# A GRU recurrence: the kept share on GpSimd, gates by the sigmoid, one joined low half, and another order of TensorE's products

## The chip, the cores and the metric

The program runs on one core of a Trainium2 chip. The metric is the device time of one execution in microseconds (us), lower is better. TensorE's granted clock is given as a share of full speed: 1.00 is 2.4 GHz, 0.50 is 1.2 GHz.

## The reference, cut to what matters

The whole reference is four layers one after the other, each added to its input: a GRU scan, an attention layer, a layer of experts and a second attention layer. Only the GRU scan is touched by the change. It walks over 196 places (14 x 14) in order, with 16 images and 192 channels at each:

```python
def step(h, xz):
    h_zrn = h @ Wh.T + bh
    x_z, x_r, x_n = jnp.split(xz, 3, axis=-1)
    h_z, h_r, h_n = jnp.split(h_zrn, 3, axis=-1)
    z = jax.nn.sigmoid(x_z + h_z)
    r = jax.nn.sigmoid(x_r + h_r)
    ncand = jnp.tanh(x_n + r * h_n)
    h_new = (1.0 - z) * ncand + z * h
    return (h_new, h_new)
_, hs = jax.lax.scan(step, h0, x_zrn_t)
```

Each step needs the state of the step before, so the 196 steps form one chain.

## The kernel before

The function `gru` holds one program for each engine, and all of them loop over the T = 196 steps. The 16 images stand in the free dimension, the 192 channels in two blocks of partitions, so every elementwise tile is 128 x 32. Work on a step goes round in a ring.

TensorE adds up three sums in PSUM: `ps_r` for the reset gate, `ps_n` for the candidate, `ps_z` for the update gate. It starts them with nine products that do not depend on the state (L516 to L518), and adds the products of the state with the recurrent weights through `gate` (L499, its matmul is L502). The state is scaled and kept as fp16 parts, a high one and a low one that holds the rest. A high part costs 6 small products, a low one 4. To start early, the new state is not awaited as a whole: it is a sum of a kept share z*h and a new share (1-z)*ncand, and `ps_r` and `ps_n` take the parts of each share (KEPT_HIGH, KEPT_LOW, NEW_HIGH, NEW_LOW) as they come, while `ps_z` takes the parts of their sum (SUM_HIGH, SUM_LOW).

ScalarE forms `tr` (L557) when `r_summed` is up, `tz` (L559) when `z_summed` is up, and the candidate `n` (L561). Both gates are a tanh of half the argument, so VectorE must add 1 and halve where it uses them.

VectorE forms `rn` (L467) from `tr` and `ps_n`, `cand` (L469), then KEPT_HIGH (L474), `zc` (L475), `kept` (L476), NEW_HIGH (L479), `new` (L480), KEPT_LOW (L483), NEW_LOW (L486), SUM_HIGH (L487), the state itself (L488), SUM_LOW (L491) and half of the state (L492). All these tiles except `ps_n` are in SBUF. GpSimd has nothing to do in the loop.

Every engine works through its own list in the order of the code. Where an instruction waits for two things, the code has two waits ahead of it:

```python
dve.wait_ge(tr_ready, t + 1)
dve.wait_ge(n_summed, t + 1)
dve.scalar_tensor_tensor(rn[:, b, :], tr[:, b, :], 1.0, ps_n[:, b, :2 * B], ALU.add, ALU.mult).then_inc(rn_ready, 1)
```

Of the kernel before, what the change touches and what calls it, by code (L numbers as in the profile page):

```python
# [2232 lines left out]
```

## Time and profile before

| what | value |
|---|---|
| median of 3 runs | 1899.13 us (1893.85 to 1899.2) |
| the profiled execution, its own time | 1891.38 us |
| its span, first to last instruction | 1889.6 us |
| mean granted clock of TensorE | 0.795 |
| busy over the span: TensorE, VectorE, ScalarE, GpSimd | 79%, 70%, 50%, 39% |
| TensorE products, the group of the costliest GRU line (`ps_r`, L502) | 3920, mean 176 ns |

The shares of the whole span mix four layers. What the change can be worth has to be read from the stretch of the recurrence alone, and there from a single step, since all steps are alike.

### The profile page before, as it was taken

To read this page: it belongs to the slowest core of one execution; us is meant where nothing else is said; L and a number is where in the kernel's file an instruction comes from. 1 tells how busy PE (TensorE), PEld (TensorE's weight loads), DVE (VectorE), ACT (ScalarE), POOL (GpSimd) and SP (SyncE) were. 2 spreads that over 40 slices of the span, in tenths; PEclk is the share of its full clock that TensorE was granted. 3 is DMA by queue.
4 is the path that set the end of the run, shared out by engine and by line. 5 is a ranking of instruction groups with operands and counts; after the bars stand their busy time and mean duration, and the time that the engine had idled before them with its cause. 6 is when DMAs were issued, how large, how long until landed. Compare 5 with 4: busy or idle time off the path is not lost. (4 is left out here: it accounts for less than half of the span.)

```text
span 1889.6 us, 51642 instructions
## 1 busy us (share of the span) xinstructions
PE 1499.0 (79%) x19499; PEld 1285.8 (68%) x19499; DVE 1322.3 (70%) x4846; ACT 952.1 (50%) x1920; POOL 740.8 (39%) x676
## 2 busy tenths in 40 slices
PE   4778888888853888888877799599992597887887
PEld 4667777777743776767666577488881586676766
DVE  7888888888867567878766765244446746787874
ACT  4633333333333567878725235244432456787872
POOL 3700000000004056869843013355540415686994
PEclk9955555555576899999985699799995689999998
DMA  3000000000022696767325214322215459676832
GB/s 83 4 4 4 4 5 4 4 4 5 4 67 85 168 246 133 158 129 148 58 59 167 77 40 163 113 64 65 65 56 158 132 148 241 136 157 126 150 58 59
DMA packets 62927, 167.59 MB, mean 89 GB/s; under 512 B 16680, under 2 KB 40344, under 8 KB 59996
## 3 DMA queue, kind: packets, MB, share of 16 engines
q1 hardware_dynamic: 57308, 151.44, 32.2%
q0 software_dynamic: 5376, 12.85, 2.3%
q8 instruction: 159, 2.61, 0.6%
q14 instruction: 84, 0.69, 0.1%
HBM read 96.24 MB, written 67.42 MB: 87 GB/s over the span
## 5 line engine op out<-in xcount | busy, mean ns | idle before, releaser
L983 POOL TENSOR_TENSOR l_arena<-l_arena,l_arena 98x784 fp32r<-98x784 f32 x192 | 354.7, 1860 | 113.3 <-PE l_ps L1092 69.6
L502 PE MATMUL gru_ps_r<-gru_hp,gru_wp 128*128 128x16 f16 x3920 | 200.5, 176 | 70.4 <-DVE gru_hp L474 69.6
L502 PEld LDWEIGHTS gru_ps_r<-gru_hp,gru_wp 128*128 128x128 f16 x3920 | 150.9, 105 | 92.0 <-DVE gru_hp L474 90.0
L922 POOL MEMSET l_arena<- 32x6272 f32 x2 | 10.6, 5320 | 513.0 <-POOLq L45 513.0
L1266 DVE TENSOR_REDUCE l_ps<-l_ps 98x4 f32<-98x784 f32 x192 | 187.5, 977 | 28.1 <-PE l_ps L1053 23.0
L502 PE MATMUL gru_ps_n<-gru_hp,gru_wp 128*128 128x16 f16 x3920 | 191.2, 174 | 0.0
L1091 PE MATMUL l_ps<-l_arena,l_arena 128*66 128x196 f32 x768 | 163.6, 266 | 25.0 <-POOL l_arena L983 24.7
L557 ACT ACTIVATE gru_tr<-gru_ps_r,gru_unscale 128x32 f32<-128x32 f32 x196 | 56.4, 288 | 220.5 <-PE gru_ps_r L502 220.5
L1206 ACT ACTIVATE l_arena<-l_ps 98x784 fp32r<-98x784 f32 x192 | 158.4, 825 | 4.6
L1209 ACT ACTIVATE l_arena<-l_ps 98x784 f32<-98x784 f32 x192 | 157.0, 818 | 0.0
L1092 PE MATMUL l_ps<-l_arena,l_arena 128*66 128x196 f32 x768 | 156.8, 257 | 0.0
L502 PEld LDWEIGHTS gru_ps_n<-gru_hp,gru_wp 128*128 128x128 f16 x3920 | 150.0, 104 | 0.0
L1197 ACT ACTIVATE l_arena<-l_ps 2x392 fp32r<-2x392 f32 x192 | 94.1, 490 | 100.7 <-PE l_ps L1062 94.3
L1053 PE MATMUL l_ps<-l_arena,l_arena 128*98 128x196 f32 x768 | 113.8, 272 | 33.2 <-DMA l_arena<-l_arena 18.9
L1091 PEld LDWEIGHTS l_ps<-l_arena,l_arena 128*66 128x66 f32 x768 | 107.5, 140 | 43.9 <-POOL l_arena L983 31.6
L1053 PEld LDWEIGHTS l_ps<-l_arena,l_arena 128*98 128x98 f32 x768 | 87.1, 171 | 52.0 <-DVE l_mt L1273 25.3
L1240 DVE COPY l_arena<-l_ps 64x196 f32<-64x196 f32 x192 | 67.6, 352 | 61.5 <-PE l_ps L1092 58.7
L1092 PEld LDWEIGHTS l_ps<-l_arena,l_arena 128*66 128x66 f32 x768 | 108.2, 141 | 1.2
L1074 PE MATMUL l_ps<-l_arena,l_arena 128*98 128x196 f32 x768 | 104.1, 259 | 0.0
L2043 DVE TENSOR_TENSOR l_arena<-mx_ps,l_arena 128x512 fp32r<-128x512 f32 x56 | 38.7, 692 | 79.2 <-ACT l_arena L1875 75.8
L1693 POOL DMA_INDIRECT picked<-l_arena,mx_target x56 | 55.3, 987 | 93.2 <-DVE l_arena L2049 93.2
L1038 PE MATMUL l_ps<-l_arena,l_arena 128*56 128x224 f32 x168 | 60.0, 357 | 38.2 <-DVE l_arena L1232 35.5
(365 smaller groups left out, 4649.3 us busy)
## 6 DMA issues: line engine op xcount, KB each, us to landing
l_arena<-qk SPq DMA_DIRECT2D x48, 588.0 KB
qk<-l_arena SPq DMA_DIRECT2D x48, 392.0 KB, 6.9
rel<-l_arena SPq DMA_DIRECT2D x24, 686.0 KB
l_arena<-rel SPq DMA_DIRECT2D x24, 686.0 KB
l_arena<-x SPq DMA_DIRECT2D x32, 294.0 KB, 7.6
qk<-l_arena SPq DMA_DIRECT2D x12, 784.0 KB, 14.2
l_arena<-in_experts_dram SPq DMA_DIRECT2D x8, 1152.0 KB, 7.5
l_arena<-picked SPq DMA_DIRECT2D x16, 294.0 KB
```

The lines of the kernel that those rows point to most:

```text
L502: last = pe.matmul(out[:, b, B * m:B * m + B], wp[:, wi, g, m, :], hp[:, b, part, B * k:B * k + B], start=False, stop=True, skip_group_che ...
L983: pool.tensor_tensor(pl[:TH, g % 2, :, :], p32[:TH, g % 2, :, :], ph[:TH, g % 4, :, :].bitcast(f32), ALU.subtract).then_inc(pl_ready, 1)
L1038: pe.matmul(out, rh[:, n, :], line(high), start=True, stop=False)
L1053: last = pe.matmul(ps[:TH, S_BANK + head, half * T:half * T + T], q[:, head, queries], k[:, head, keys], start=True, stop=True)
L1074: last = pe.matmul(ps[:TH, T_BANK + 2 * (g % 2) + head, half * T:half * T + T], k[:, head, keys], q[:, head, queries], start=True, stop=True)
L1091: pe.matmul(out, values, ph[:, g % 4, head, cols], start=head == 0 and keys == 0, stop=False)
L1092: last = pe.matmul(out, values, pl[:, g % 2, head, cols], start=False, stop=head == 1 and keys == 1)
L1197: act.activation(q[0:2, :, b * T:(b + 1) * T], ps[64:66, R_BANK, :TB].rearrange("p (h t) -> p h t", h=2), ACT.Copy).then_inc(x_copied, 1)
L1206: act.activation(ph[:TH, g % 4, :, :], banks, ACT.Exp).then_inc(p_high, 1)
L1209: act.activation(p32[:TH, g % 2, :, :], banks, ACT.Exp).then_inc(p_ready, 1)
L1240: dve.tensor_copy(o_quad[p // 2][row:row + 64, b * T:(b + 1) * T], ps[:64, O_BANK, :T]).then_inc(o_kept, 1)
L1266: dve.tensor_reduce(m, ps[:TH, S_BANK:S_BANK + 2, :TB].rearrange("p c (h k) -> p c h k", h=2), AXIS.X, ALU.max).then_inc(mx_ready, 1)
```

## The change

In the loop of `gru`, five things change.

- ScalarE forms the gates `reset` and `keep` by the sigmoid in place of tanh. VectorE no longer adds 1 and halves; `unscale` loses its factor of one half, and the tile `half` becomes `held`, the whole state.
- GpSimd forms the kept share `kept` (a product of `keep` and the state) and its rest KEPT_LOW. VectorE did both before.
- For the candidate's sum the two low parts are added to a single part, BOTH_LOW, by a new VectorE instruction; TensorE multiplies it once (4 products) where it multiplied KEPT_LOW and NEW_LOW (8 products).
- `renew` (formerly `zc`), `new` and `held` (formerly `half`) lie in PSUM, in a bank of their own called `shares`.
- TensorE's products come in another order.

```diff
-        hp = s.sb("hp", [128, 2, 6, 2 * B], fp16)
+        hp = s.sb("hp", [128, 2, 7, 2 * B], fp16)
...
-        tr, tz, zc, rn, cand, tn, kept, new, half = (s.sb(n, [128, 2, 2 * B]) for n in names)
+        reset, keep, rn, cand, tn, kept = (s.sb(n, [128, 2, 2 * B]) for n in names)
...
+        shares = s.ps("shares", 1)[:, 0, :12 * B].rearrange("p (a b n) -> p a b n", a=3, b=2)
+        renew, new, held = (shares[:, a] for a in range(3))
...
-                    dve.wait_ge(tr_ready, t + 1)
+                    dve.wait_ge(reset_ready, t + 1)
                     dve.wait_ge(n_summed, t + 1)
-                    dve.scalar_tensor_tensor(rn[:, b, :], tr[:, b, :], 1.0, ps_n[:, b, :2 * B], ALU.add, ALU.mult).then_inc(rn_ready, 1)
+                    dve.tensor_tensor(rn[:, b, :], reset[:, b, :], ps_n[:, b, :2 * B], ALU.mult).then_inc(rn_ready, 1)
...
-                    dve.wait_ge(tz_ready, t + 1)
-                    dve.wait_ge(half_ready, t + 1)
-                    dve.scalar_tensor_tensor(hp[:, 1 - b, KEPT_HIGH, :], tz[:, b, :], 1.0, half[:, b, :], ALU.add, ALU.mult).then_inc(kept_high, 1)
-                    dve.tensor_scalar(zc[:, b, :], tz[:, b, :], -0.5 * HSCALE, 0.5 * HSCALE, ALU.mult, ALU.add).then_inc(zc_ready, 1)
-                    dve.scalar_tensor_tensor(kept[:, b, :], tz[:, b, :], 1.0, half[:, b, :], ALU.add, ALU.mult).then_inc(kept_ready, 1)
-                    dve.wait_ge(zc_ready, t + 1)
+                    dve.wait_ge(keep_ready, t + 1)
+                    dve.wait_ge(held_ready, t + 1)
+                    dve.tensor_tensor(hp[:, 1 - b, KEPT_HIGH, :], keep[:, b, :], held[:, b, :], ALU.mult).then_inc(kept_high, 1)
+                    dve.tensor_scalar(renew[:, b, :], keep[:, b, :], -HSCALE, HSCALE, ALU.mult, ALU.add).then_inc(renew_ready, 1)
+                    dve.wait_ge(renew_ready, t + 1)
                     dve.wait_ge(tn_ready, t + 1)
-                    dve.tensor_tensor(hp[:, 1 - b, NEW_HIGH, :], zc[:, b, :], tn[:, b, :], ALU.mult).then_inc(new_high, 1)
-                    dve.tensor_tensor(new[:, b, :], zc[:, b, :], tn[:, b, :], ALU.mult).then_inc(new_ready, 1)
-                    dve.wait_ge(kept_high, t + 2)
-                    dve.wait_ge(kept_ready, t + 1)
-                    dve.tensor_tensor(hp[:, 1 - b, KEPT_LOW, :], kept[:, b, :], hp[:, 1 - b, KEPT_HIGH, :], ALU.subtract).then_inc(kept_low, 1)
+                    dve.tensor_tensor(hp[:, 1 - b, NEW_HIGH, :], renew[:, b, :], tn[:, b, :], ALU.mult).then_inc(new_high, 1)
+                    dve.tensor_tensor(new[:, b, :], renew[:, b, :], tn[:, b, :], ALU.mult).then_inc(new_ready, 1)
                     dve.wait_ge(new_high, t + 2)
                     dve.wait_ge(new_ready, t + 1)
                     dve.tensor_tensor(hp[:, 1 - b, NEW_LOW, :], new[:, b, :], hp[:, 1 - b, NEW_HIGH, :], ALU.subtract).then_inc(new_low, 1)
+                    dve.wait_ge(kept_ready, t + 1)
                     dve.tensor_tensor(hp[:, 1 - b, SUM_HIGH, :], new[:, b, :], kept[:, b, :], ALU.add).then_inc(sum_high, 1)
                     dve.tensor_tensor(state[:, t + 1, :, :], two(new[:, b, :]), two(kept[:, b, :]), ALU.add).then_inc(h_ready, 1)
+                    dve.wait_ge(new_low, t + 2)
+                    dve.wait_ge(kept_low, t + 2)
+                    dve.tensor_tensor(hp[:, 1 - b, BOTH_LOW, :], hp[:, 1 - b, KEPT_LOW, :], hp[:, 1 - b, NEW_LOW, :], ALU.add).then_inc(both_low, 1)
...
-                    dve.tensor_scalar(two(half[:, 1 - b, :]), state[:, t + 1, :, :], 0.5, None, ALU.mult).then_inc(half_ready, 1)
+                    dve.tensor_tensor(held[:, 1 - b, :], new[:, b, :], kept[:, b, :], ALU.add).then_inc(held_ready, 1)
...
                     gate(ps_r, 1, b, NEW_HIGH)
-                    gate(ps_n, 2, b, NEW_HIGH)
                     pe.wait_ge(kept_low, t + 1)
                     gate(ps_r, 1, b, KEPT_LOW)
+                    gate(ps_n, 2, b, NEW_HIGH, [0])
                     pe.wait_ge(new_low, t + 1)
                     gate(ps_r, 1, b, NEW_LOW).then_inc(r_summed, 1)
-                    gate(ps_n, 2, b, KEPT_LOW)
-                    gate(ps_n, 2, b, NEW_LOW).then_inc(n_summed, 1)
+                    gate(ps_n, 2, b, NEW_HIGH, [1])
                     pe.wait_ge(sum_high, t + 1)
                     gate(ps_z, 0, b, SUM_HIGH)
+                    pe.wait_ge(both_low, t + 1)
+                    gate(ps_n, 2, b, BOTH_LOW).then_inc(n_summed, 1)
                     pe.wait_ge(sum_low, t + 1)
...
+                for t in range(T):
+                    b = t % 2
+                    pool.wait_ge(h_ready, t + 1)
+                    pool.wait_ge(keep_ready, t + 1)
+                    pool.tensor_tensor(two(kept[:, b, :]), two(keep[:, b, :]), state[:, t, :, :], ALU.mult).then_inc(kept_ready, 1)
+                    pool.wait_ge(kept_high, t + 2)
+                    pool.wait_ge(kept_ready, t + 1)
+                    pool.tensor_tensor(hp[:, 1 - b, KEPT_LOW, :], kept[:, b, :], hp[:, 1 - b, KEPT_HIGH, :], ALU.subtract).then_inc(kept_low, 1)
...
-                    act.activation(tr[:, b, :], ps_r[:, b, :2 * B], ACT.Tanh, scale=unscale[:, 0:1]).then_inc(tr_ready, 1)
+                    act.activation(reset[:, b, :], ps_r[:, b, :2 * B], ACT.Sigmoid, scale=unscale[:, 0:1]).then_inc(reset_ready, 1)
...
-                    act.activation(tz[:, b, :], ps_z[:, b, :2 * B], ACT.Tanh, scale=unscale[:, 0:1]).then_inc(tz_ready, 1)
+                    act.activation(keep[:, b, :], ps_z[:, b, :2 * B], ACT.Sigmoid, scale=unscale[:, 0:1]).then_inc(keep_ready, 1)
```

TensorE, one step, the products that depend on the state, before. In this code `x6` stands for six products in a row; they are in turn KEPT_HIGH for both sums, NEW_HIGH for both, then both low parts for `ps_r` (x8), both low parts for `ps_n` (x8), and the sum's parts for `ps_z` (x10).

```order
L502 MATMUL gru_ps_r<-gru_hp,gru_wp 128x16 x6
L502 MATMUL gru_ps_n<-gru_hp,gru_wp 128x16 x6
L502 MATMUL gru_ps_r<-gru_hp,gru_wp 128x16 x6
L502 MATMUL gru_ps_n<-gru_hp,gru_wp 128x16 x6
L502 MATMUL gru_ps_r<-gru_hp,gru_wp 128x16 x8
L502 MATMUL gru_ps_n<-gru_hp,gru_wp 128x16 x8
L502 MATMUL gru_ps_z<-gru_hp,gru_wp 128x16 x10
```

The same place after the change. The `x10` are NEW_HIGH (6) and KEPT_LOW (4), the `x4` behind the first `x3` is NEW_LOW, and the last `ps_n` group is BOTH_LOW.

```order
L504 MATMUL gru_ps_r<-gru_hp,gru_wp 128x16 x6
L504 MATMUL gru_ps_n<-gru_hp,gru_wp 128x16 x6
L504 MATMUL gru_ps_r<-gru_hp,gru_wp 128x16 x10
L504 MATMUL gru_ps_n<-gru_hp,gru_wp 128x16 x3
L504 MATMUL gru_ps_r<-gru_hp,gru_wp 128x16 x4
L504 MATMUL gru_ps_n<-gru_hp,gru_wp 128x16 x3
L504 MATMUL gru_ps_z<-gru_hp,gru_wp 128x16 x6
L504 MATMUL gru_ps_n<-gru_hp,gru_wp 128x16 x4
L504 MATMUL gru_ps_z<-gru_hp,gru_wp 128x16 x4
```

Between the last product of `ps_r` and the last of `ps_n` there stood 8 products, and now there stand 13. The count of a step goes from 50 to 46.

VectorE, one step from KEPT_HIGH on, before:

```order
L474 SCALAR_TENSOR_TENSOR gru_hp<-gru_tz,gru_half 128x32
L475 TENSOR_SCALAR gru_zc<-gru_tz 128x32
L476 SCALAR_TENSOR_TENSOR gru_kept<-gru_tz,gru_half 128x32
L479 TENSOR_TENSOR gru_hp<-gru_zc,gru_n 128x32
L480 TENSOR_TENSOR gru_new<-gru_zc,gru_n 128x32
L483 TENSOR_TENSOR gru_hp<-gru_kept,gru_hp 128x32
L486 TENSOR_TENSOR gru_hp<-gru_new,gru_hp 128x32
L487 TENSOR_TENSOR gru_hp<-gru_new,gru_kept 128x32
L488 TENSOR_TENSOR l0s_state<-gru_new,gru_kept 128x32
L491 TENSOR_TENSOR gru_hp<-l0s_state,gru_hp 128x32
L492 TENSOR_SCALAR gru_half<-l0s_state 128x32
```

And after (`gru_shares` is the PSUM tile with `renew`, `new` and `held`; L490 is BOTH_LOW):

```order
L476 TENSOR_TENSOR gru_hp<-gru_keep,gru_shares 128x32
L477 TENSOR_SCALAR gru_shares<-gru_keep 128x32
L480 TENSOR_TENSOR gru_hp<-gru_shares,gru_n 128x32
L481 TENSOR_TENSOR gru_shares<-gru_shares,gru_n 128x32
L484 TENSOR_TENSOR gru_hp<-gru_shares,gru_hp 128x32
L486 TENSOR_TENSOR gru_hp<-gru_shares,gru_kept 128x32
L487 TENSOR_TENSOR l0s_state<-gru_shares,gru_kept 128x32
L490 TENSOR_TENSOR gru_hp<-gru_hp 128x32
L493 TENSOR_TENSOR gru_hp<-l0s_state,gru_hp 128x32
L494 TENSOR_TENSOR gru_shares<-gru_shares,gru_kept 128x32
```

`kept` and KEPT_LOW have left the list, and BOTH_LOW has come in between the state and SUM_LOW.

## Rows read from the trace of the kernel before

**Rows 1.** Busy time by stretch: recurrence, and the stage ahead; x counts instructions

```profile
core 0: us, PE busy (x) PEld busy (x) DVE busy (x) ACT busy (x) POOL busy (x), PEclk, DMA share, GB/s
107.00:530.00 423.00, 351.00 (x11425) 329.06 (x11422) 363.77 (x2527) 155.42 (x582) 0.00 (x0) 0.50 0.02 4
...
0.00:90.00 90.00, 56.16 (x292) 53.39 (x292) 71.17 (x195) 48.43 (x98) 49.42 (x38) 0.99 0.16 44
```

**Rows 2.** Waits, 110 to 530 us: total, times, longest

```profile
ACT gru_tr L557 <- PE gru_ps_r L502: 214.6, 193, 1.4
```

**Rows 3.** Timeline of VectorE over one step: start us, length us

```profile
507.20 0.19 DVE L479 TENSOR_TENSOR gru_hp<-gru_zc,gru_n 128x32 f16<-128x32 f32 x1
507.31 0.19 DVE L480 TENSOR_TENSOR gru_new<-gru_zc,gru_n 128x32 f32<-128x32 f32 x1
...
507.60 0.19 DVE L486 TENSOR_TENSOR gru_hp<-gru_new,gru_hp 128x32 f16<-128x32 f32 x1
...
507.81 0.18 DVE L488 TENSOR_TENSOR l0s_state<-gru_new,gru_kept 128x32 f32<-128x32 f32 x1
508.10 0.19 DVE L491 TENSOR_TENSOR gru_hp<-l0s_state,gru_hp 128x32 f16<-128x32 f32 x1
...
508.51 0.19 DVE L467 SCALAR_TENSOR_TENSOR gru_rn<-gru_tr,gru_ps_n 128x32 f32<-128x32 f32 x1
508.74 0.25 DVE L469 SCALAR_TENSOR_TENSOR gru_cand<-gru_rn,gru_unscale,l0g_cand_in 128x32 f32<-128x32 f32 x1
508.99 0.19 DVE L474 SCALAR_TENSOR_TENSOR gru_hp<-gru_tz,gru_half 128x32 f16<-128x32 f32 x1
...
509.36 0.19 DVE L479 TENSOR_TENSOR gru_hp<-gru_zc,gru_n 128x32 f16<-128x32 f32 x1
```

**Rows 4.** Timeline of TensorE's weight loads, one row of the step

```profile
507.44 0.24 PEld L502 LDWEIGHTS gru_ps_r<-gru_hp,gru_wp 128*128 128x128 f16 x6
```

**Rows 5.** Timeline of TensorE's products, same step: first start, length to last end

```profile
507.45 0.33 PE L502 MATMUL gru_ps_r<-gru_hp,gru_wp 128*128 128x16 f16 x6
507.63 0.31 PE L502 MATMUL gru_ps_n<-gru_hp,gru_wp 128*128 128x16 f16 x6
507.79 0.36 PE L502 MATMUL gru_ps_r<-gru_hp,gru_wp 128*128 128x16 f16 x8
508.01 0.36 PE L502 MATMUL gru_ps_n<-gru_hp,gru_wp 128*128 128x16 f16 x8
508.22 0.41 PE L502 MATMUL gru_ps_z<-gru_hp,gru_wp 128*128 128x16 f16 x10
508.49 0.19 PE L516 MATMUL gru_ps_r<-l0g_gates_in,gru_ident 128*128 128x32 bf16 x1
```

**Rows 6.** Timeline of ScalarE, same step, with idle time and releaser

```profile
508.19 0.29 ACT L557 ACTIVATE gru_tr<-gru_ps_r,gru_unscale 128x32 f32<-128x32 f32 x1 [1.10 <-PE gru_ps_r L502]
508.67 0.29 ACT L559 ACTIVATE gru_tz<-gru_ps_z,gru_unscale 128x32 f32<-128x32 f32 x1 [0.19 <-PE gru_ps_z L502]
509.02 0.23 ACT L561 ACTIVATE gru_n<-gru_cand 128x32 f32<-128x32 f32 x1
```

**Rows 7.** Timeline of GpSimd in a later layer, two dependent instructions

```profile
735.23 0.21 POOL L967 CAST l_rec_parts<-l_sums 98x32 fp32r<-98x32 f32 x1
735.52 0.25 POOL L969 TENSOR_TENSOR l_rec_parts<-l_sums,l_rec_parts 98x32 fp32r<-98x32 f32 x1
```

**Rows 8.** Groups by shape: busy us, mean ns, idle before

```profile
L961 POOL TENSOR_TENSOR l_arena<-l_arena,l_arena 98x128 fp32r<-98x128 f32 x96 | 40.3, 440 | 0.0
...
L1431 ACT ACTIVATE ro_std<-ro_var_sums,ro_eps 128x32 f32<-128x32 f32 x1 | 0.3, 287 | 6.7 <-PE ro_var_sums L1406 6.7
```

**Rows 9.** VectorE groups by shape, inputs in SBUF, then one in PSUM

```profile
L1901 DVE TENSOR_TENSOR mx_key<-l_logits,mx_m 98x256 f32<-98x256 f32 x2 | 0.8, 425 | 0.1
...
L1932 DVE TENSOR_TENSOR mx_pos<-mx_ps,mx_base_slot 98x256 f32<-98x256 f32 x1 | 0.4, 424 | 0.0
```

**Rows 10.** Line 168: min/median/max ns; result in SBUF, then in PSUM

```profile
L168 DVE TENSOR_SCALAR l_arena<-l_arena,l_arena x64: 364/375/3690, 591.3 to 1513.6; 96x196 f32<-96x196 f32 x64
L168 DVE TENSOR_SCALAR gi_xn<-l_x,gi_rstd,gi_shift x32: 453/473/493, 21.8 to 73.6; 96x196 f32<-96x196 f32 x32
```

More of the change, by code:

```diff
@@ L388, in gru @@
         bp, br = s.sb("bp", [128, 3, 2, B], bf16), s.sb("br", [128, 2, B])
-        hp = s.sb("hp", [128, 2, 6, 2 * B], fp16)
-        KEPT_HIGH, KEPT_LOW, NEW_HIGH, NEW_LOW, SUM_HIGH, SUM_LOW = range(6)
-        names = "tr tz zc rn cand n kept new half".split()
-        tr, tz, zc, rn, cand, tn, kept, new, half = (s.sb(n, [128, 2, 2 * B]) for n in names)
+        hp = s.sb("hp", [128, 2, 7, 2 * B], fp16)
+        KEPT_HIGH, KEPT_LOW, NEW_HIGH, NEW_LOW, SUM_HIGH, SUM_LOW, BOTH_LOW = range(7)
+        names = "reset keep rn cand n kept".split()
+        reset, keep, rn, cand, tn, kept = (s.sb(n, [128, 2, 2 * B]) for n in names)
         ps_r, ps_n, ps_z = s.ps("ps_r", 2), s.ps("ps_n", 2), s.ps("ps_z", 2)
+        shares = s.ps("shares", 1)[:, 0, :12 * B].rearrange("p (a b n) -> p a b n", a=3, b=2)
+        renew, new, held = (shares[:, a] for a in range(3))
         wo_raw = s.sb("wo_raw", [128, 2, CB, CP])
@@ L400, in gru @@
         kept_high, kept_low, new_high, new_low = (s.sem(n) for n in ("kept_high", "kept_low", "new_high", "new_low"))
-        h_ready, half_ready, sum_high, sum_low = (s.sem(n) for n in ("h_ready", "half_ready", "sum_high", "sum_low"))
+        h_ready, held_ready, sum_high, sum_low, both_low = (s.sem(n) for n in ("h_ready", "held_ready", "sum_high", "sum_low", "both_low"))
         r_summed, n_summed, z_summed = s.sem("r_summed"), s.sem("n_summed"), s.sem("z_summed")
-        tr_ready, tz_ready, tn_ready = s.sem("tr_ready"), s.sem("tz_ready"), s.sem("tn_ready")
-        zc_ready, rn_ready, cand_ready = s.sem("zc_ready"), s.sem("rn_ready"), s.sem("cand_ready")
+        reset_ready, keep_ready, tn_ready = s.sem("reset_ready"), s.sem("keep_ready"), s.sem("tn_ready")
+        renew_ready, rn_ready, cand_ready = s.sem("renew_ready"), s.sem("rn_ready"), s.sem("cand_ready")
         kept_ready, new_ready = s.sem("kept_ready"), s.sem("new_ready")
@@ L420, in _ @@
                 dve.memset(state[:, 0, :, :], 0.0).then_inc(h_ready, 1)
-                dve.memset(half[:, 0, :], 0.0).then_inc(half_ready, 1)
+                dve.memset(held[:, 0, :], 0.0).then_inc(held_ready, 1)
                 for part, ready in ((KEPT_HIGH, kept_high), (KEPT_LOW, kept_low), (NEW_HIGH, new_high), (NEW_LOW, new_low),
-                                    (SUM_HIGH, sum_high), (SUM_LOW, sum_low)):
+                                    (SUM_HIGH, sum_high), (SUM_LOW, sum_low), (BOTH_LOW, both_low)):
                     dve.memset(hp[:, 0, part, :], 0.0).then_inc(ready, 1)
@@ L440, in _ @@
                 link(dve.tensor_scalar(power[:, :].bitcast(mybir.dt.uint32), largest[:, :].bitcast(mybir.dt.uint32), 0x7F800000, None, ALU.bitwise_and))
-                link(dve.tensor_scalar(unscale[:, :], power[:, :], 0.5 / HSCALE * 2.0 ** -13, None, ALU.mult))
+                link(dve.tensor_scalar(unscale[:, :], power[:, :], 1.0 / HSCALE * 2.0 ** -13, None, ALU.mult))
                 dve.reciprocal(scale[:, :], power[:, :]).then_inc(scale_ready, 1)
@@ L497, in _, with gate @@
                 LOW = [(0, 0), (2, 1)]
-                def gate(out, g, b, part):
-                    for m in range(2):
+                def gate(out, g, b, part, halves=range(2)):
+                    for m in halves:
                         for wi, k in HIGH if part in (KEPT_HIGH, NEW_HIGH, SUM_HIGH) else LOW:
```

## The prediction

> **What bounds the kernel now.** I first read busy time by stretch. The recurrence lasts from 107 to 530 us, 423 us of the span, or 2.16 us for each of 196 steps; TensorE has its lower clock all through (0.50, 1.2 GHz) and is busy 351 us of it, so no engine is full [rows 1]. The waits then say who waits: ScalarE waits for the reset gate's sums, 1.1 us in each of 193 steps [rows 2]. That is a ring, not a full engine, so I read one step of the timeline and followed the ring from NEW_HIGH (L479) to the next NEW_HIGH. All times below are us after the start of NEW_HIGH at 507.20.
>
> - NEW_HIGH ends at 0.19 [rows 3]; TensorE's weight load for it starts at 0.24 [rows 4], the first product at 0.25.
> - 20 products later (6 + 6 + 8) the sums of `ps_r` end at 0.95 (507.79 + 0.36) [rows 5].
> - ScalarE starts `tr` at 0.99 and ends it at 1.28 [rows 6]; `rn` starts at 1.31, `cand` at 1.54 and ends at 1.79 [rows 3]; `n` starts at 1.82 and ends at 2.05 [rows 6]; the next NEW_HIGH starts at 2.16 [rows 3], or 2.15 without the rounding.
>
> Nothing on this ring stands idle: each starts 0.03 to 0.11 after the end of the one before. The other branches come out close behind. `rn` also needs the candidate's sums, which end at 1.17 (508.01 + 0.36) [rows 5]. The gate `tz` ends at 1.76, and KEPT_HIGH starts at 1.79 [rows 6, 3]; its 12 products are through just before NEW_HIGH is there.
>
> Three prices for the sum. Products follow at 0.027 (from 507.63 to 508.49 there are 6 + 8 + 8 + 10 = 32 of them in 0.86), the first group after a pause takes about 0.02 more (507.45 to 507.63 against 507.63 to 507.79), and a product ends 0.17 to 0.18 after its start (the last of the 6 that begin at 507.63 starts 0.135 later and ends at 0.31) [rows 5]. Independent VectorE instructions start 0.10 to 0.11 apart. A dependent one starts 0.04 after its producer's end if it has one wait (`rn` ends 508.70, `cand` 508.74), but 0.10 to 0.11 if it has two and the one written second comes last (`new` ends 507.50, L486 starts 507.60; L488 ends 507.99, L491 starts 508.10) [rows 3]. `rn` before waits for `tr` first and `n_summed` second, and the second is there long ahead, so it starts 0.03 after `tr`.
>
> **The change, part by part.**
>
> *Products.* 4 fewer in a step would be 0.11 us if TensorE were full. It isn't; what counts is where the last product of each sum stands. NEW_HIGH is ready for TensorE at 0.24 as before. Then come 6 + 4 + 3 products, and the weight load for NEW_LOW could be at about 0.25 + 0.02 + 13 x 0.027 = 0.62, less a little since loads run ahead: 0.60. NEW_LOW itself: `new` starts 0.11, ends 0.30, plus 0.10 for the second wait, plus 0.19 is 0.59, plus 0.05 to the load is 0.64. So TensorE now pauses 0.04 there, where 20 products covered it before. The products of NEW_LOW start at 0.65 and, with 0.02 for the restart, 4 of them put the next one at 0.78; the last ends at 0.75 + 0.17 = 0.92 to 0.93. The reset gate is ready 0.02 to 0.03 earlier than before: `reset` ends 0.96 + 0.29 = 1.25, and `rn` could start at 1.28.
>
> *The candidate's sums.* Behind the last product of `ps_r` now stand 3 + 6 + 4 = 13 products in place of 8. They end at 0.93 + 13 x 0.027 = 1.28, against 1.17. BOTH_LOW doesn't delay them: VectorE reaches it at 0.40 + 0.11 + 0.10 + 0.10 = 0.71, it ends at 0.90, is ready for TensorE at 0.95, and its turn is at 0.78 + 9 x 0.027 = 1.02. Now `n_summed` is the last wait of `rn`, and it is written second: 1.28 + 0.10 = 1.38. Against 1.31 that is **+0.07 us a step**. Before, the same edge would have given 1.17 + 0.10 = 1.27, 0.04 ahead of the reset gate: the cover was thin, and the five products use it up. The price of the second wait is bounded by the rows at 0.04 and 0.11; I take 0.10, since it is the same form of code.
>
> *Sigmoid for tanh.* No sigmoid of this shape runs before. Another function at 128 x 32 from PSUM, the square root, takes 287 ns [rows 8], as the tanh's 0.29 [rows 6], so I take no difference. If it took 0.05 more, `reset` would be ready at 1.33, still inside 1.38. `rn` becomes a product of two tensors, no shorter on VectorE (0.18 to 0.19 for either kind) [rows 3].
>
> *GpSimd.* `keep` ends at about 1.75: the state starts 0.21 after NEW_LOW's 0.40, ends at 0.79, and SUM_LOW with its second wait (0.10), 0.19 and 0.05 is there for TensorE at 1.13; the last of its 4 products ends at 1.42, then 0.04 and 0.29. GpSimd forms `kept` from perhaps 1.87 to 2.12 (0.25 for 98 x 32; 0.08 from one dependent instruction to the next) and KEPT_LOW from 2.20 to 2.45 [rows 7]. With 0.05 it is ready at 2.50; its turn in a step of 2.22 is at 2.22 + 0.24 + 0.18 = 2.64. So it is hidden with 0.14 to spare under the products of the state. VectorE's two instructions less save nothing, as it had gaps. If each took the 440 ns of a 98 x 128 tile [rows 8], KEPT_LOW would be 0.24 late and cost up to that a step; the near row is the 98 x 32 one, so I take nothing.
>
> *Tiles in PSUM.* Only `new` and what reads it lie on the path. A PSUM input costs nothing for a product of two tensors: 424 ns against 425 at 98 x 256 [rows 9]. A PSUM result does for L168, 473 ns against 375 [rows 10]. If that were a fixed price, `new` would be 0.10 later; if it goes by columns (196 there, 32 here) it is 0.016. I take nothing, as that line has one tensor input and `new` has two. The Trainium skill, VectorE: DVE Perf Modes, section on the perf-mode tier table, says that fp32 `tensor_scalar` runs at twice the rate in SBUF only, while `tensor_tensor` has the single rate in either memory. By that rule L168's 98 ns are the lost rate and `new` pays nothing; by the row read as a fixed price the sum would be +0.17 a step.
>
> *The sum.* 0.07 us x 196 = 13.7 us, made against the profiled execution's own 1891.4 us: 1905.1. That execution lies 7.7 us under the median of the runs, 1899.1; on the median the forecast is **1912.8 us**. Rounding of the rows (0.01 at three joints) is worth 2 us either way. Other layers aren't touched.
>
> **The rivals.**
>
> 1. *The candidate's edge is cheaper, and the change is a wash.* If `new` is done 0.04 earlier in PSUM, TensorE doesn't pause: all 30 products to the last of `ps_n` run from 0.25, ending at 0.25 + 0.02 + 29 x 0.027 + 0.17 = 1.22, and `rn` starts at 1.32, +0.01: 1901. If only the second wait costs 0.04, `rn` starts at 1.32 too. For it: both are thin margins. Against: rows show 0.10 twice, and no PSUM result that was faster. Chance 0.18, 1895 to 1904.
> 2. *Faster.* VectorE's instructions with a PSUM operand are shorter throughout. It decides once NEW_HIGH, with `renew` now in PSUM, is at least 0.015 shorter and `new` and NEW_LOW together 0.05: then the whole run of products moves up. With 0.06 off each of the three, the products begin at 0.19, `rn` starts at 1.26, and with `rn` itself 0.02 shorter a step is 0.07 less: 1885. Against it: the pair of 424 and 425 ns. Chance 0.18, 1880 to 1893.
> 3. *Much slower.* GpSimd is late, or `new` pays the 0.10 of L168. Either gives some 0.10 more a step, 1932. For it: no GpSimd row has this shape with waits on two other engines, and its instructions sit in the ring of KEPT_LOW, `ps_r` and `keep`. Against: 0.14 of slack. Chance 0.14, 1920 to 1945.
>
> The same page of the skill, section on the TRN2 errata, gives VectorE a fixed part of 120 cycles from PSUM and 58 from SBUF. By it `new` and NEW_LOW would each take 62 cycles at 0.96 GHz, 65 ns, longer, an estimate of +0.13 a step on top of mine, in rival 3's direction; the pair of 424 and 425 ns disagrees, and rival 3 would keep its chance without it.
>
> **How the numbers follow.** The forecast has a chance of 0.50, with 1904 to 1920 as its own range (second wait 0.07 to 0.11, rounding, some of the columns' 0.016). A measurement here tells no change from change beyond 0.3%, 5.7 us or 0.03 us a step. Slower is then 0.50 + 0.14 = 0.64, same 0.18, faster 0.18. The range from 1893 to 1928 takes in the forecast and the wash and most of a GpSimd that is only a little late, and leaves out the faster case and the worst of the third.
>
> **What would show it.** In the timeline of a step: the period 2.22 us in place of 2.15; the last product of `ps_n` ending 0.35 after the last of `ps_r` (0.22 before); `rn` starting 0.13 after `reset` ends, not 0.03, and VectorE's idle time ahead of it put down to TensorE, not to ScalarE; a pause of 0.04 ahead of NEW_LOW's products; the recurrence 13 to 14 us longer, and everything behind it as before. `new` at 0.19, the sigmoid at 0.29, GpSimd's two at 0.25 each would confirm the prices. I am wrong if `new` or NEW_HIGH is clearly shorter in PSUM, if `rn` starts within 0.05 of the candidate's sums, if TensorE's first wait after NEW_HIGH is on GpSimd, or if the clock in the stretch isn't 0.50.

## The result, and the profile after

The changed kernel takes 1908.94 us, the median of 9 runs (1904.54 to 1914.37); the kernel before, run beside it, 1893.85 us (9 runs, 1888.44 to 1899.2). The ratio is 1.008 with a 95% interval of 1.0061 to 1.0098, so it is slower by 0.8%, 15 us. The forecast was slower by 0.07 us a step, 13.7 us; its 1912.8 us is counted from 1899.13, the median of 3 runs of the kernel before.

The profiled execution spans 1907.1 us at a mean clock of 0.791. Where does the length lie? One instruction stands once in each of the 196 steps, `rn`. This view gives its shortest, median and longest duration in ns, and its first and last start in us; the line under it says how long VectorE sat idle ahead of it, how often, and for whom. It counts only pauses above 0.15 us.

```profile
L469 DVE TENSOR_TENSOR gru_rn<-gru_reset,gru_ps_n x196: 178/188/189, 104.5 to 542.0; 128x32 f32<-128x32 f32 x196
its engine sat idle before it (us, times) until:
  PE gru_ps_n L504: 37.1, 190
```

The same view of the kernel before:

```profile
L467 DVE SCALAR_TENSOR_TENSOR gru_rn<-gru_tr,gru_ps_n x196: 180/186/190, 103.5 to 528.1; 128x32 f32<-128x32 f32 x196
its engine sat idle before it (us, times) until:
  ACT gru_tr L557: 2.6, 4
```

From the first `rn` to the last are 437.5 us after and 424.6 before: 12.9 us more in 195 steps, 0.066 a step. The counts of 190 and 4 say who was awaited, but not how much longer: the pause before was 0.13 us in the typical step, just too short to be counted. The groups by shape give all of VectorE's idle time ahead of `rn` in the recurrence (the number behind the second bar), before and after:

```profile
L467 DVE SCALAR_TENSOR_TENSOR gru_rn<-gru_tr,gru_ps_n 128x32 f32<-128x32 f32 x193 | 36.1, 187 | 24.4 <-ACT gru_tr L557 0.7
L469 DVE TENSOR_TENSOR gru_rn<-gru_reset,gru_ps_n 128x32 f32<-128x32 f32 x193 | 36.2, 188 | 35.3 <-PE gru_ps_n L504 35.0
```

It rose from 0.13 to 0.18 us a step, and now it ends with TensorE's candidate sums.

The busy time by stretch, in the columns of [rows 1], first the recurrence, then a stretch of the untouched layers:

```profile
107.00:543.00 436.00, 364.10 (x10661) 333.07 (x10661) 335.05 (x2333) 156.06 (x584) 97.27 (x390) 0.50 0.02 4
...
887.00:1187.00 300.00, 260.14 (x1421) 198.65 (x1419) 206.18 (x483) 141.19 (x238) 125.84 (x117) 0.80 0.36 99
```

and the matching later stretch of the kernel before:

```profile
873.00:1173.00 300.00, 254.07 (x1430) 194.59 (x1429) 208.56 (x484) 143.29 (x241) 125.19 (x117) 0.83 0.35 98
```

In the recurrence the granted clock is 0.50, as in [rows 1], so the clock has no part in the 12.9 us. The spans differ by 17.5 us: 12.9 in the steps, 1.0 ahead of the first `rn`, and 3.6 behind the last, where nothing was changed and one execution had 0.80 where the other had 0.83. Those 3.6 us can't be put down to the change: in the profiled executions of this document, all with the same later layers, the stretch behind the last `rn` takes from 1358.6 to 1372.1 us. Between the medians of 9 runs the difference is 15.1.

One step of the changed kernel on VectorE, in the columns of [rows 3]; a bracket gives the idle time ahead and what ended it:

```profile
507.07 0.19 DVE L480 TENSOR_TENSOR gru_hp<-gru_shares,gru_n 128x32 f16<-128x32 f32 x1 [0.17 <-ACT gru_n L572]
507.18 0.19 DVE L481 TENSOR_TENSOR gru_shares<-gru_shares,gru_n 128x32 f32<-128x32 f32 x1
507.47 0.19 DVE L484 TENSOR_TENSOR gru_hp<-gru_shares,gru_hp 128x32 f16<-128x32 f32 x1
...
507.77 0.16 DVE L490 TENSOR_TENSOR gru_hp<-gru_hp 128x32 f16<-128x32 f16 x1
...
508.45 0.19 DVE L469 TENSOR_TENSOR gru_rn<-gru_reset,gru_ps_n 128x32 f32<-128x32 f32 x1 [0.18 <-PE gru_ps_n L504]
508.67 0.25 DVE L471 SCALAR_TENSOR_TENSOR gru_cand<-gru_rn,gru_unscale,l0g_cand_in 128x32 f32<-128x32 f32 x1
...
509.29 0.19 DVE L480 TENSOR_TENSOR gru_hp<-gru_shares,gru_n 128x32 f16<-128x32 f32 x1 [0.15 <-ACT gru_n L572]
```

TensorE's products of the step, in the columns of [rows 5]:

```profile
507.32 0.44 PE L504 MATMUL gru_ps_r<-gru_hp,gru_wp 128*128 128x16 f16 x10
507.61 0.23 PE L504 MATMUL gru_ps_n<-gru_hp,gru_wp 128*128 128x16 f16 x3
507.72 0.28 PE L504 MATMUL gru_ps_r<-gru_hp,gru_wp 128*128 128x16 f16 x4
507.85 0.23 PE L504 MATMUL gru_ps_n<-gru_hp,gru_wp 128*128 128x16 f16 x3
507.93 0.31 PE L504 MATMUL gru_ps_z<-gru_hp,gru_wp 128*128 128x16 f16 x6
508.09 0.25 PE L504 MATMUL gru_ps_n<-gru_hp,gru_wp 128*128 128x16 f16 x4
```

ScalarE and GpSimd in the same step:

```profile
508.03 0.29 ACT L568 ACTIVATE gru_reset<-gru_ps_r,gru_unscale 128x32 f32<-128x32 f32 x1 [1.07 <-PE gru_ps_r L504]
508.53 0.29 ACT L570 ACTIVATE gru_keep<-gru_ps_z,gru_unscale 128x32 f32<-128x32 f32 x1 [0.21 <-PE gru_ps_z L504]
508.96 0.23 ACT L572 ACTIVATE gru_n<-gru_cand 128x32 f32<-128x32 f32 x1
```

```profile
508.96 0.25 POOL L555 TENSOR_TENSOR gru_kept<-gru_keep,l0s_state 128x32 f32<-128x32 f32 x1 [1.61 <-ACT gru_keep L570]
509.35 0.25 POOL L558 TENSOR_TENSOR gru_hp<-gru_kept,gru_hp 128x32 f16<-128x32 f32 x1
```

The step is 2.22 us long (509.29 less 507.07), as in the median over the recurrence, against 2.15. The last product of `ps_r` ends at 508.00 (507.72 + 0.28), the last of `ps_n` at 508.34 (508.09 + 0.25): 0.34 behind it. `reset` ends at 508.32, and `rn` starts at 508.45, 0.13 later and 0.11 behind the candidate's sums. The reset gate alone would have let it go at 508.35, 0.03 behind its end, as `rn` started behind `tr` before [rows 3, 6].

### The profile page after: what moved, and what is told of

Same layout as the page of the kernel before. It is cut to its first block and busy times, and to the rows that moved or that the text cites. A ratio compares the mean times of both kernels' runs of the same rounds, so it can differ in the third digit from the quotient of the medians.

```text
span 1907.1 us, 50662 instructions
## 1 busy us (share of the span) xinstructions
PE 1518.7 (80%) x18715; PEld 1292.6 (68%) x18715; DVE 1291.4 (68%) x4651; ACT 952.9 (50%) x1920; POOL 839.7 (44%) x1068
## 5 line engine op out<-in xcount | busy, mean ns | idle before, releaser
L504 PE MATMUL gru_ps_n<-gru_hp,gru_wp 128*128 128x16 f16 x3136 | 199.1, 174 | 0.0
L555 POOL TENSOR_TENSOR gru_kept<-gru_keep,l0s_state 128x32 f32<-128x32 f32 x196 | 49.6, 253 | 322.7 <-ACT gru_keep L570 322.7
L568 ACT ACTIVATE gru_reset<-gru_ps_r,gru_unscale 128x32 f32<-128x32 f32 x196 | 56.4, 288 | 214.3 <-PE gru_ps_r L504 214.3
L504 PEld LDWEIGHTS gru_ps_n<-gru_hp,gru_wp 128*128 128x128 f16 x3136 | 144.2, 104 | 0.5
L504 PE MATMUL gru_ps_z<-gru_hp,gru_wp 128*128 128x16 f16 x1960 | 109.8, 176 | 0.7 <-DVE gru_hp L493 0.7
```

What stands on the lines that cost most here:

```text
L504: last = pe.matmul(out[:, b, B * m:B * m + B], wp[:, wi, g, m, :], hp[:, b, part, B * k:B * k + B], start=False, stop=True, skip_group_che ...
L568: act.activation(reset[:, b, :], ps_r[:, b, :2 * B], ACT.Sigmoid, scale=unscale[:, 0:1]).then_inc(reset_ready, 1)
```

## The experiments

Three explanations had to be told apart. By the prediction's, `rn` waits for the candidate's sums, which now come 13 products behind those of the reset gate, and the wait for them is written second, which costs 0.10 in place of 0.04. Or the loss lies in the other parts (GpSimd, sigmoid, PSUM). Or the late sums are the cause, but by their lateness alone, and where their wait is written costs nothing of its own. The first four kernels ran beside a kernel before with a median of 1893.46 us, the last four beside one of 1894.69 us. "A typical step" is the median over the recurrence of one profiled execution. Before: 2.15, after: 2.22.

### e1: the order undone

The changed kernel with TensorE's order of before and without BOTH_LOW; GpSimd, the sigmoid and the PSUM tiles stay.

```diff
-                    dve.wait_ge(new_low, t + 2)
-                    dve.wait_ge(kept_low, t + 2)
-                    dve.tensor_tensor(hp[:, 1 - b, BOTH_LOW, :], hp[:, 1 - b, KEPT_LOW, :], hp[:, 1 - b, NEW_LOW, :], ALU.add).then_inc(both_low, 1)
...
                     gate(ps_r, 1, b, NEW_HIGH)
+                    gate(ps_n, 2, b, NEW_HIGH)
                     pe.wait_ge(kept_low, t + 1)
                     gate(ps_r, 1, b, KEPT_LOW)
-                    gate(ps_n, 2, b, NEW_HIGH, [0])
                     pe.wait_ge(new_low, t + 1)
                     gate(ps_r, 1, b, NEW_LOW).then_inc(r_summed, 1)
-                    gate(ps_n, 2, b, NEW_HIGH, [1])
+                    gate(ps_n, 2, b, KEPT_LOW)
+                    gate(ps_n, 2, b, NEW_LOW).then_inc(n_summed, 1)
                     pe.wait_ge(sum_high, t + 1)
                     gate(ps_z, 0, b, SUM_HIGH)
-                    pe.wait_ge(both_low, t + 1)
-                    gate(ps_n, 2, b, BOTH_LOW).then_inc(n_summed, 1)
```

> The changed kernel with the products' order of before and without BOTH_LOW (both low parts are multiplied for the candidate's sum again); sigmoid, GpSimd's share and the tiles in PSUM stay. Theory (the place of the candidate's last product is the whole loss): a step of 2.15 to 2.16 us as before, rn 0.03 after reset, ratio to before 0.998 to 1.002. Rival (GpSimd, the tiles in PSUM or the sigmoid carry a good part of the loss): a step of 2.18 to 2.22 us, ratio 1.004 to 1.008.

Measured: 1895.74 us, ratio to before 1.0004 (0.9981 to 1.0027), a typical step 2.146 us. The view of `rn`:

```profile
L469 DVE TENSOR_TENSOR gru_rn<-gru_reset,gru_ps_n x196: 186/187/189, 105.3 to 527.2; 128x32 f32<-128x32 f32 x196
its engine sat idle before it (us, times) until:
  ACT gru_reset L564: 1.7, 1
```

From first to last are 421.9 us, 2.7 less than before, with GpSimd, the sigmoid and PSUM all in place. They cost nothing that shows within the interval, 0.3% at most. The whole loss goes with the order and BOTH_LOW.

### e2: the order alone

The kernel before with the new order of products and BOTH_LOW on VectorE; tanh, `half`, SBUF tiles and `kept` on VectorE stay.

```diff
+                    dve.wait_ge(new_low, t + 2)
+                    dve.wait_ge(kept_low, t + 2)
+                    dve.tensor_tensor(hp[:, 1 - b, BOTH_LOW, :], hp[:, 1 - b, KEPT_LOW, :], hp[:, 1 - b, NEW_LOW, :], ALU.add).then_inc(both_low, 1)
...
-                    gate(ps_n, 2, b, NEW_HIGH)
...
+                    gate(ps_n, 2, b, NEW_HIGH, [0])
...
-                    gate(ps_n, 2, b, KEPT_LOW)
-                    gate(ps_n, 2, b, NEW_LOW).then_inc(n_summed, 1)
+                    gate(ps_n, 2, b, NEW_HIGH, [1])
...
+                    pe.wait_ge(both_low, t + 1)
+                    gate(ps_n, 2, b, BOTH_LOW).then_inc(n_summed, 1)
```

> The kernel before with the new order of products and with BOTH_LOW on VectorE; tanh, kept and KEPT_LOW on VectorE and all tiles in SBUF stay. Theory: the whole loss, a step of 2.22 us, rn 0.10 after the last product of the candidate's sum ends, ratio to before 1.006 to 1.008. Rival (the loss is in the other parts): a step of 2.15 to 2.18 us, ratio under 1.004.

Measured: 1909.46 us, ratio 1.0084 (1.0061 to 1.0108), a typical step 2.22 us.

```profile
L467 DVE SCALAR_TENSOR_TENSOR gru_rn<-gru_tr,gru_ps_n x196: 179/186/190, 103.4 to 540.9; 128x32 f32<-128x32 f32 x196
its engine sat idle before it (us, times) until:
  PE gru_ps_n L505: 39.4, 188
```

437.5 us from first to last, the very length of the changed kernel, and the same wait in 188 steps. The ratio lies a hair above the expected 1.006 to 1.008, which its interval reaches. With e1 this settles where the loss is, and the explanation by the other parts falls.

### e3: the candidate's low part ahead of the update gate

The changed kernel with BOTH_LOW's products in front of SUM_HIGH's, so that 7 products stand behind the last of `ps_r` and not 13.

```diff
+                    pe.wait_ge(both_low, t + 1)
+                    gate(ps_n, 2, b, BOTH_LOW).then_inc(n_summed, 1)
                     pe.wait_ge(sum_high, t + 1)
                     gate(ps_z, 0, b, SUM_HIGH)
-                    pe.wait_ge(both_low, t + 1)
-                    gate(ps_n, 2, b, BOTH_LOW).then_inc(n_summed, 1)
```

> The changed kernel with the 4 products of BOTH_LOW ahead of the 6 of SUM_HIGH. Theory: BOTH_LOW is ready for TensorE 0.92 us after NEW_HIGH, so TensorE pauses there for 0.04, the candidate's sums end at 1.20 in place of 1.27, rn starts at 1.31; a step of 2.15 to 2.17 us (the update gate comes 0.05 later and may cost up to 0.015 through KEPT_LOW on GpSimd), ratio to before 0.999 to 1.003. Rival (the loss is not in the distance from the reset gate's last product to the candidate's): still 2.20 us or more, ratio 1.006 or more.

Measured: 1896.74 us, ratio 1.0008 (0.9988 to 1.0027), a typical step 2.15 us. Two rows of TensorE and `rn` in one step, from two timelines:

```profile
402.46 0.28 PE L504 MATMUL gru_ps_r<-gru_hp,gru_wp 128*128 128x16 f16 x4
402.59 0.42 PE L504 MATMUL gru_ps_n<-gru_hp,gru_wp 128*128 128x16 f16 x7
...
403.11 0.19 DVE L469 TENSOR_TENSOR gru_rn<-gru_reset,gru_ps_n 128x32 f32<-128x32 f32 x1
```

The sums of `ps_n` end 0.27 behind those of `ps_r` (403.01 and 402.74). Moving six products past four took the loss away with everything else left as it was. `rn` still starts 0.10 to 0.11 behind the candidate's sums, the price of the wait written second, but that is now only 0.04 behind the end of `reset` in the median (0.03 before, 0.13 in the changed kernel).

### e4: one wait for `rn`

The changed kernel, with both of `rn`'s producers raising one semaphore, so that there is a single wait.

```diff
-                    dve.wait_ge(reset_ready, t + 1)
-                    dve.wait_ge(n_summed, t + 1)
+                    dve.wait_ge(rn_inputs, 2 * t + 2)
...
-                    gate(ps_n, 2, b, BOTH_LOW).then_inc(n_summed, 1)
+                    gate(ps_n, 2, b, BOTH_LOW).then_inc(rn_inputs, 1)
...
-                    act.activation(reset[:, b, :], ps_r[:, b, :2 * B], ACT.Sigmoid, scale=unscale[:, 0:1]).then_inc(reset_ready, 1)
+                    act.activation(reset[:, b, :], ps_r[:, b, :2 * B], ACT.Sigmoid, scale=unscale[:, 0:1]).then_inc(rn_inputs, 1)
```

> The changed kernel with one semaphore for both inputs of rn (the reset gate and the candidate's sums both count it up, and rn waits once for the even value); nothing else changes. Theory (0.06 to 0.07 us of the loss is the price of the second of two waits): rn starts 0.04 after the candidate's sums end, or 0.03 after reset ends if that is later, at 1.31 in place of 1.38 after NEW_HIGH; a step of 2.15 to 2.16 us, ratio 0.998 to 1.002. Rival (0.10 is the time that any wait of VectorE for TensorE takes): no change against the changed kernel, a step of 2.22 us, ratio 1.007.

Measured: 1891.55 us, ratio 0.9989 (0.9972 to 1.0006), a typical step 2.15 us. The last product of `ps_n` and `rn` in one step, from two timelines of this kernel:

```profile
403.42 0.25 PE L503 MATMUL gru_ps_n<-gru_hp,gru_wp 128*128 128x16 f16 x4
...
403.71 0.19 DVE L468 TENSOR_TENSOR gru_rn<-gru_reset,gru_ps_n 128x32 f32<-128x32 f32 x1
```

The order is the slow one and the sums are as late as ever, ending at 403.67 (in the median 0.35 behind those of `ps_r`, as in the changed kernel); but `rn` starts 0.04 behind them, not 0.11. The kernel gains all of the 0.07 us back. So the loss has two conditions, and taking either away heals it: the sums must be last, and their wait must be the one written second. Lateness alone doesn't explain it.

### e5: the two waits of `rn` swapped

```diff
-                    dve.wait_ge(reset_ready, t + 1)
                     dve.wait_ge(n_summed, t + 1)
+                    dve.wait_ge(reset_ready, t + 1)
```

> The changed kernel with the two waits of rn in the other order: the candidate's sums first, reset second. Theory (the wait written second costs 0.10 from its producer's end, the one written first 0.04): rn starts 0.04 after the candidate's sums (1.31) or 0.10 after reset ends (1.25 + 0.10 = 1.35 to 1.36), whichever is later, so 1.36 and 0.10 after reset; a step of 2.20 us, ratio to before 1.004 to 1.006. Rival (the price is that of having two waits, in either order): rn stays at 1.38, a step of 2.22 us, ratio 1.007 to 1.008.

Measured: 1903.46 us, ratio 1.0042 (1.0022 to 1.0062), a typical step 2.19 us. The reset gate and `rn` in one step:

```profile
403.36 0.29 ACT L568 ACTIVATE gru_reset<-gru_ps_r,gru_unscale 128x32 f32<-128x32 f32 x1 [1.06 <-PE gru_ps_r L504]
...
403.75 0.19 DVE L469 TENSOR_TENSOR gru_rn<-gru_reset,gru_ps_n 128x32 f32<-128x32 f32 x1 [0.16 <-PE gru_ps_n L504]
```

The swap brings back 0.03 of the 0.07, and no more, because both inputs come within 0.02 of each other. In the compiled program the wait written second is an instruction of its own, ahead of `rn` in VectorE's queue; where its input is the late one, the trace records it 0.065 us before the instruction that it guards. Now it waits for the reset gate, which ends at 403.65, and `rn` follows at 403.75, 0.10 later. The bracket names TensorE here, since its sums ended 0.01 after the gate, yet with the waits this way round it is the gate that `rn` hangs on: a releaser named by the view is the input that came last, which isn't always the one that held the instruction.

### e6: every late wait alone or first

The changed kernel with e4's edit, the same for NEW_HIGH (whose inputs are `renew` and `n`), and the waits swapped where the late one was second: NEW_LOW, SUM_LOW, and GpSimd's KEPT_LOW. The order of products stays the slow one.

```diff
-                    dve.wait_ge(renew_ready, t + 1)
-                    dve.wait_ge(tn_ready, t + 1)
+                    dve.wait_ge(new_inputs, 2 * t + 2)
...
-                    dve.wait_ge(new_high, t + 2)
                     dve.wait_ge(new_ready, t + 1)
+                    dve.wait_ge(new_high, t + 2)
...
-                    dve.wait_ge(sum_high, t + 2)
                     dve.wait_ge(h_ready, t + 2)
+                    dve.wait_ge(sum_high, t + 2)
...
-                    pool.wait_ge(kept_high, t + 2)
                     pool.wait_ge(kept_ready, t + 1)
+                    pool.wait_ge(kept_high, t + 2)
```

> The changed kernel, its order of products kept; rn and NEW_HIGH wait once each on a shared semaphore, and NEW_LOW, SUM_LOW and KEPT_LOW on GpSimd have the wait that comes last written first. Theory: 0.06 to 0.07 us less at each of rn, NEW_HIGH and NEW_LOW, as far as another branch does not hold: NEW_HIGH 0.03 after n ends, NEW_LOW 0.04 after new ends, no pause of TensorE ahead of NEW_LOW; a step of 2.03 to 2.09 us, ratio to before 0.987 to 0.994. Rival (some engine is nearly full, so the time comes back elsewhere): a step of 2.13 us or more, ratio over 0.997.

Measured: 1866.22 us, ratio 0.9852 (0.9828 to 0.9876), a typical step 2.03 us, at the fast end of what was expected and a little past it in the ratio. VectorE's timeline, one step:

```profile
403.15 0.19 DVE L478 TENSOR_TENSOR gru_hp<-gru_shares,gru_n 128x32 f16<-128x32 f32 x1
403.26 0.19 DVE L479 TENSOR_TENSOR gru_shares<-gru_shares,gru_n 128x32 f32<-128x32 f32 x1
403.49 0.19 DVE L482 TENSOR_TENSOR gru_hp<-gru_shares,gru_hp 128x32 f16<-128x32 f32 x1
...
404.41 0.19 DVE L468 TENSOR_TENSOR gru_rn<-gru_reset,gru_ps_n 128x32 f32<-128x32 f32 x1 [0.20 <-PE gru_ps_n L502]
```

ScalarE's `n` ahead of it:

```profile
402.89 0.23 ACT L570 ACTIVATE gru_n<-gru_cand 128x32 f32<-128x32 f32 x1
```

`n` ends at 403.12 and NEW_HIGH starts 0.03 later, where it was 0.10 in the kernel after (509.19 and 509.29). `new` ends at 403.45 and NEW_LOW starts 0.04 later, where it was 0.10 (507.37 and 507.47). So TensorE has NEW_LOW 0.07 earlier, the pause ahead of it goes, and `rn` stands 1.26 behind NEW_HIGH, where it was 1.38. Three joints on the ring are 0.07 shorter each. At `rn` and at NEW_HIGH the step gains all of it; at NEW_LOW it gains only what TensorE's pause and its restart had cost, some 0.05. Together that is 0.19, and the step is 0.19 shorter than after (2.027 against 2.220).

### e7: the same for the kernel before

Here the early input of `rn` is already the one written second, so its waits stay as they are, and so do those of KEPT_LOW.

```diff
-                    dve.wait_ge(zc_ready, t + 1)
-                    dve.wait_ge(tn_ready, t + 1)
+                    dve.wait_ge(new_inputs, 2 * t + 2)
...
-                    dve.wait_ge(new_high, t + 2)
                     dve.wait_ge(new_ready, t + 1)
+                    dve.wait_ge(new_high, t + 2)
...
-                    dve.wait_ge(sum_high, t + 2)
                     dve.wait_ge(h_ready, t + 2)
+                    dve.wait_ge(sum_high, t + 2)
```

> The kernel before, its order of products kept; NEW_HIGH waits once for zc and n on a shared semaphore, NEW_LOW and SUM_LOW have the late wait written first. Theory: NEW_HIGH starts 0.03 after n ends in place of 0.10; what holds next is TensorE, whose 12 products of KEPT_HIGH for both sums end only 0.04 before NEW_HIGH's come, so the step loses 0.04 and not 0.07: 2.11 us, ratio 0.994 to 0.997. Rival: TensorE's products do not hold, 0.07 less, 2.08 us, ratio 0.993 or less.

Measured: 1886.05 us, ratio 0.9947 (0.9929 to 0.9966), a typical step 2.11 us. NEW_HIGH on VectorE, and TensorE's products of KEPT_HIGH (the first two groups) and of NEW_HIGH (the other two):

```profile
403.02 0.19 DVE L478 TENSOR_TENSOR gru_hp<-gru_zc,gru_n 128x32 f16<-128x32 f32 x1
...
402.96 0.33 PE L501 MATMUL gru_ps_r<-gru_hp,gru_wp 128*128 128x16 f16 x6 [0.35 <-DVE gru_hp L474]
403.14 0.31 PE L501 MATMUL gru_ps_n<-gru_hp,gru_wp 128*128 128x16 f16 x6
403.30 0.31 PE L501 MATMUL gru_ps_r<-gru_hp,gru_wp 128*128 128x16 f16 x6
403.46 0.31 PE L501 MATMUL gru_ps_n<-gru_hp,gru_wp 128*128 128x16 f16 x6
```

The same second group in the kernel before, ahead of the 507.45 of [rows 5]:

```profile
507.27 0.31 PE L502 MATMUL gru_ps_n<-gru_hp,gru_wp 128*128 128x16 f16 x6
```

The step is 0.04 shorter and not 0.07, for the reason that was expected. NEW_HIGH ends at 403.21, but its products start at 403.30, 0.09 later, where it was 0.06 before: they follow the group ahead at the plain pace of six products (403.14 to 403.30, 0.16; before 0.18, with a pause and a restart). So TensorE's twelve products of KEPT_HIGH hold the ring now. From their first to the last of `ps_z` all 50 products follow each other without a pause, 1.33 us between first and last start in the median step. The last product (0.17), the joint to the gate (0.04), `tz` (0.29), the joint to KEPT_HIGH (0.03), KEPT_HIGH (0.19) and the joint to its first product (0.06) make that up to 2.11, the whole step. An earlier NEW_LOW buys nothing either, since 16 products stand ahead of its own.

Set beside e6 this turns the verdict on the change round. With the late waits mended, the changed kernel is 20 us faster than the kernel before (1866.22 against 1886.05). In e6 the same run of products is 46 long and takes 1.25 us, 0.08 less, and the step is 0.08 shorter too. The four products that the change takes out of a step are 0.11 at 0.027 each, less some 0.03 for what is left of a pause and a restart ahead of NEW_HIGH's. What the order or GpSimd's share are worth by themselves with the waits mended was not tried.

### e8: mended waits and a new order

e6, with half of the candidate's NEW_HIGH ahead of KEPT_LOW and BOTH_LOW between the halves of SUM_HIGH.

```diff
                     gate(ps_r, 1, b, NEW_HIGH)
+                    gate(ps_n, 2, b, NEW_HIGH, [0])
                     pe.wait_ge(kept_low, t + 1)
                     gate(ps_r, 1, b, KEPT_LOW)
-                    gate(ps_n, 2, b, NEW_HIGH, [0])
...
-                    gate(ps_z, 0, b, SUM_HIGH)
+                    gate(ps_z, 0, b, SUM_HIGH, [0])
                     pe.wait_ge(both_low, t + 1)
                     gate(ps_n, 2, b, BOTH_LOW).then_inc(rn_inputs, 1)
+                    gate(ps_z, 0, b, SUM_HIGH, [1])
```

> As the changed kernel with all late waits alone (one wait for rn and for NEW_HIGH, late wait first elsewhere), and in addition an order of products that puts half of the candidate's NEW_HIGH products ahead of KEPT_LOW, and BOTH_LOW between the halves of SUM_HIGH. Theory: KEPT_LOW from GpSimd is no longer awaited, the candidate's last product follows the reset gate's by 10, not 13; a step of 2.01 to 2.04 us, ratio to before 0.984 to 0.989, the fastest of all. Rival: GpSimd's two instructions or the 12 products of KEPT_HIGH hold the step at 2.08 us or more, no better than without the new order.

Measured: 1860.66 us, ratio 0.9807 (0.9785 to 0.9829), a typical step 2.007 us, both a little under what was expected. Its median is the lowest of the ten kernels; its interval just touches e6's.

```profile
L468 DVE TENSOR_TENSOR gru_rn<-gru_reset,gru_ps_n x196: 186/188/189, 105.0 to 496.3; 128x32 f32<-128x32 f32 x196
its engine sat idle before it (us, times) until:
  ACT gru_reset L567: 35.2, 196
```

In all 196 steps `rn` now waits for the reset gate: the candidate's sums are off the ring, and the 391.3 us from first to last are 33 us less than before. TensorE's 46 products from KEPT_HIGH on take 1.23 us from first to last start, 0.02 less than in e6, and the step is 0.02 shorter: as in e7, it is the run of products through the update gate that fills the step.

## Why the prediction held

**The ring and the edge that took it over: right.** The last wait of `rn` became the candidate's sums, as the text said, and VectorE's idle time ahead of it is now put down to TensorE. The sums ended 0.34 behind those of `ps_r` (0.35 forecast), `rn` started 0.13 behind `reset` (0.13), and the step grew by 0.066 in the mean and 0.069 in the typical step (0.07). e2 shows that the order and BOTH_LOW alone make this, e1 that nothing else does.

**The price of a second wait: right, and now shown.** It was taken from two places in the trace of before; e4 takes it away and the loss goes.

**The pause ahead of NEW_LOW: right.** In the step shown NEW_LOW's first product starts at 507.72, and the three ahead of it would have been through at 507.69; 0.03, in this step and in the median one (0.04 forecast).

**The prices taken as nothing.** The sigmoid takes 288 ns, as the tanh's 0.29 [rows 6]. `new` takes 189 ns into PSUM, where it was 0.19 [rows 3], so the 98 ns of [rows 10] did not carry over. By the Trainium skill, VectorE: DVE Perf Modes, section on the perf-mode tier table, an fp32 `tensor_tensor` has the single rate in SBUF and in PSUM alike; with that the trace agrees. NEW_HIGH, reading `renew` from PSUM, takes 192 ns and took 0.19 before [rows 3]. By the same page of the Trainium skill, section on the TRN2 errata, a VectorE instruction from PSUM has a fixed part 62 cycles longer than one from SBUF, an estimate of 65 ns; with that the trace does not agree. The pair of [rows 9] on which the price of a PSUM input rested is a comparison and an addition, not two products; NEW_HIGH is the product that bears it out.

**GpSimd: hidden, but by less than was said.** Its two take 253 and 246 ns in the median, as estimated from [rows 7]. But `kept` starts 0.14 behind the end of `keep` (508.82 and 508.96) and KEPT_LOW 0.14 behind `kept` (509.21 and 509.35), where the sum had 0.12 and 0.08: both have two waits. KEPT_LOW ends at 509.60, and with the 0.05 to the load it is ready at 509.65; its turn is 0.42 behind NEW_HIGH, at 509.71. The spare was 0.06, not 0.14, and the rival in which GpSimd is late was nearer than the prediction took it to be. With its waits swapped in e6, KEPT_LOW starts 0.08 behind `kept`.

**The sum.** 0.066 for 195 steps is 12.9 us against 13.7; the medians of the runs differ by 15.1, and the interval (11.6 to 18.6 us) holds both. The remainder is not resolved. The time itself, 1908.94, came in 3.9 us under the forecast of 1912.8, because the kernel before had a median of 1893.85 over 9 runs and not the 1899.13 of 3 runs from which the forecast was counted; the slowdown was 1.4 us larger than forecast.

**What stays open.** Some steps are over 0.06 us longer than the median: 28 of 195 before, 24 after, 20 to 28 in e1 to e5, 13 in e7, and none at all in e6 and e8. The view of waits gives a few of them to "issue", time in which the engine waited for nothing that the profile shows. They are 2 to 5 us in all, and their going accounts for most of why e6 gained 27.6 us on e4 from first `rn` to last, while 0.126 a typical step makes 24.6. That they go where the late waits are mended is what was seen; why was not tested. Nor was it tried which of e6's swaps does how much.

## What to carry to other kernels

In a ring of short instructions, ask of each instruction with two inputs which comes last, and let its wait be the only one (a shared semaphore) or the first written: each such joint here was 0.07 us shorter for it, and in the changed kernel the step took 2.03 us in place of 2.22. When the order of work on an engine is changed, count what now stands between the last piece of each sum and the sum that closes the ring: five products more there cost 0.07 us, and the four products fewer in a step bought nothing until the joints were mended. And a change that measures slower may be a good one held up by something small: undo its parts one at a time, mend the joint, and time it again before it is dropped.

## What the runs showed of the hardware

- On VectorE an instruction started 0.03 to 0.04 us after its last input if that was its only wait or the first written, and 0.10 to 0.11 if it was the one written second (`rn` in after, e4 and e5; NEW_HIGH and NEW_LOW in after and e6). On GpSimd KEPT_LOW started 0.14 us after `kept` with that wait second and 0.08 with it first (after, e6).
- GpSimd took 253 and 246 ns for a product and a difference of 128x32 that VectorE does in 0.18 to 0.19.
- A VectorE addition with both inputs and the result in fp16 (BOTH_LOW) took 165 ns, against 180 to 193 ns for the additions, products and subtractions with an fp32 input at the same shape.
- Results and inputs in PSUM made no difference beyond 5 ns to a VectorE product of two 128x32 tensors (`new` 184 before and 189 after, NEW_HIGH 193 and 192).
- At a granted clock of 0.50 TensorE's products of 128x16 followed each other every 0.027 us, 50 of them in a row in e7, and the first behind a pause cost some 0.02 more.
